# An attention kernel whose Gram rows are scaled by their diagonal, with the low parts of the diagonal blocks kept in one triangle

## What is computed

```python
q = heads(x @ W_q); k_t = heads(text_ehs @ W_k); v_t = heads(text_ehs @ W_v)
probs_t = softmax(einsum('bhsd,bhtd->bhst', q, k_t) * attn_scale)
text_out = einsum('bhst,bhtd->bhsd', probs_t, v_t)
qsem = l2norm(einsum('bhst,bte->bhse', probs_t, text_ehs))
sem = einsum('bhse,bne->bhsn', qsem, l2norm(ip_ehs))
probs_ip = softmax(q @ k_ip * attn_scale + 0.5 * sem) * spatial_mask
out = (text_out + probs_ip @ v_ip) @ W_out + b_out + x
```

## Time and profile before

| | us |
|---|---|
| median of 3 runs | 434.62 |
| lowest, highest | 431.41, 434.82 |
| the profiled execution | 431.83 |
| its span, first to last instruction | 430.0 |

### The profile page before, as it was taken

The page is one execution under the profiler, slowest core; times in us unless marked ns, Lnnn a source line. Parts: engine busy times, 40 slices in busy tenths (PEclk is TensorE's granted clock), DMA queues, the critical chain, the costliest instruction groups (busy, mean ns, idle before and its releaser), DMA issues.

```text
span 430.0 us, 9498 instructions
## 1 busy us (share of the span) xinstructions
PE 401.6 (93%) x3656; PEld 322.4 (75%) x3656; DVE 224.8 (52%) x482; ACT 204.3 (47%) x483; POOL 206.3 (48%) x218
## 2 busy tenths in 40 slices
PE   8999898899899999999999999999999899986786
PEld 5648678678788878887878788878888688864652
DVE  0893773656357635652666347544566366424232
ACT  1524125364555554656445645465553654473520
POOL 3020380354547543766268624963474328438351
PEclk9999999999999999999999999999999999999795
DMA  8499895066217320571147023712072100010000
GB/s 280 126 301 187 213 169 127 11 182 104 63 68 159 57 78 2 156 125 49 31 142 139 12 69 109 147 27 78 2 169 40 38 2 3 3 37 2 2 16 13
DMA packets 29455, 38.03 MB, mean 88 GB/s; under 512 B 14361, under 2 KB 26745, under 8 KB 28729
## 3 DMA queue, kind: packets, MB, share of 16 engines
q1 hardware_dynamic: 28514, 36.36, 35.7%
q10 hardware_dynamic: 896, 1.07, 0.8%
HBM read 28.50 MB, written 8.81 MB: 87 GB/s over the span
## 4 chain that ended last, share of the span: by engine, by line
PE 84%; ACT 4%; DVE 3%; DMA 3%; POOL 2%; issue 2%; SPq 1%; ACTq 0%; POOLq 0%; DVEq 0%
PE PR L883 41%; PE Y L883 26%; PE O L883 8%; PE P L883 8%; DMA et<-ctxT 2%; ACT big L666 1%; ACT er L670 1%; POOL pb L532 1%; DVE big L751 1%; POOL t L554 1%; ACT R L685 1%; PE PR L1042 1%; DVE mx L785 1%; DMA qst<-ma 0%; DVE el L725 0%
## 5 line engine op out<-in xcount | busy, mean ns | idle before, releaser
L532 POOL TENSOR_TENSOR pb<-pb 128x448 f32<-128x448 f32 x78 | 88.8, 1139 | 134.9 <-DVE pb L807 128.8
L785 DVE TENSOR_REDUCE mx<-PR 112x1 f32<-112x371 f32 x160 | 83.8, 539 | 85.1 <-PE PR L883 84.1
L883 PE MATMUL Y<-er,Gh 128*128 128x448 f32 x240 | 96.2, 401 | 5.6 <-ACT er L670 5.6
L807 DVE TENSOR_TENSOR pb<-big,Y 128x448 f32<-128x448 f32 x120 | 73.2, 621 | 38.9 <-PE Y L883 38.9
L883 PE MATMUL Y<-er,Gl 128*128 128x448 f32 x240 | 88.1, 367 | 0.0
L666 ACT ACTIVATE big<-P 128x448 f32<-128x448 f32 x120 | 65.0, 541 | 14.9 <-PE P L883 14.2
L670 ACT ACTIVATE er<-big 128x448 fp32r<-128x448 f32 x120 | 69.3, 578 | 3.8
L883 PEld LDWEIGHTS Y<-er,Gh 128*128 128x128 f32 x240 | 45.8, 191 | 20.4 <-DVE pb L807 11.1
L883 PE MATMUL PR<-kst,qst 96*112 96x371 bf16 x160 | 51.6, 331 | 3.0 <-DVE mx L785 2.0
L883 PE MATMUL P<-qst,kst 99*128 99x112 bf16 x480 | 41.7, 215 | 6.2 <-ACT big L666 5.9
L883 PEld LDWEIGHTS Y<-er,Gl 128*128 128x128 f32 x240 | 45.8, 191 | 2.1
(11 more groups left out here) (147 smaller groups left out, 660.3 us busy)
## 6 DMA issues: line engine op xcount, KB each, us to landing
et<-ctxT SPq DMA_DIRECT2D x8, 752.0 KB, 4.6
kst<-kd SPq DMA_DIRECT2D x7, 720.0 KB, 7.4
kd<-ks SPq DMA_DIRECT2D x16, 288.0 KB, 2.9
qst<-qd SPq DMA_DIRECT2D x48, 70.0 KB, 2.5
kst<-kd SPq DMA_DIRECT2D x7, 480.0 KB, 9.3
kst<-kd SPq DMA_DIRECT2D x9, 240.0 KB, 9.3
qd<-kst SPq DMA_DIRECT2D x4, 336.0 KB, 6.1
vx<-xr SPq DMA_DIRECT2D x8, 140.0 KB, 2.2
```

Of the source, the lines that this page charges most:

```text
L532: pool.tensor_tensor(total, total, (pz, pm)[j], ALU.add).then_inc(s_S, 1)
L785: dve.tensor_reduce(mx[b % 2][:, h:h + 1], bank[0:S, 0:T], AX.X, ALU.max).then_inc(s_free[seq[u] % NR], 1)
L807: dve.tensor_tensor((pz, pm, pa[g % 2])[j], eb[g % 3][:, 448 * j:448 * j + 448], Y[y % 2][:, 0:448], ALU.mult).then_inc(s_P, 1)
L883: return pe.matmul(o, st, mv, start=start, stop=stop, **kw)
```

## The change

The diagonal of each G block is taken first (c, at least 1e-30), row k of G is divided by c_k, and er becomes round(e * c). In a diagonal block the low parts of both triangles are gathered by symmetry into one triangle, rounded into Gh itself: so diagonal blocks need no Gl, and a gram has 5 + 3 + 1 = 9 matmuls. For this a G unit has two parts on DVE: a head (diagonal by a product with the identity and a sum, clamp, reciprocal) before ACT's rounding, and a part "Gl" behind it that also writes dj, the low parts above the diagonal; GpSimd halves the diagonal and clears one triangle of Gh ("U"), PE transposes dj into a further PR bank ("D", L1002 of the new file), and DVE adds the transposed block into Gh. ROUNDS moves one m and takes U0 to U2 and D0 to D2 in. usel's entry for the norm is 2.0 instead of 1.0. ident_d grows from 128x128 to 128x384 (identity and two triangle masks).

```diff
-          "S0 m g m K2 m S1 v m S2 G1 m",
-          "S0 m g T0 T1 m r0 G2 m S1 m pw v S2 m V0",
-          "Kr S0 r1 m g m V1 m S1 m m v r2 S2 mT z V2",
+          "S0 m g m U0 K2 m S1 v m D0 S2 G1 m",
+          "S0 m g T0 T1 m r0 U1 G2 m D1 S1 pw v S2 m m V0",
+          "Kr S0 r1 U2 m g m V1 m S1 m m v r2 D2 S2 mT z V2",
...
-    order += [("G", 0, i) for i in range(3)] + [("K", 1, c) for c in range(3)] + [("Kr", 1)]
+    order += [("G", 0, 0), ("G", 0, 1), ("U", 0, 0), ("D", 0, 0), ("G", 0, 2), ("U", 0, 1), ("D", 0, 1)]
+    order += [("K", 1, 0), ("U", 0, 2), ("D", 0, 2)] + [("K", 1, c) for c in (1, 2)] + [("Kr", 1)]
...
-    order += [("mT", 0)] + [("G", 1, i) for i in range(3)] + [("St", 0, c) for c in range(3)]
+    order += [("mT", 0)] + [("G", 1, 0), ("G", 1, 1), ("U", 1, 0), ("D", 1, 0), ("G", 1, 2), ("U", 1, 1), ("D", 1, 1)]
+    order += [("St", 0, c) for c in range(3)] + [("U", 1, 2), ("D", 1, 2)]
...
+                if u[0] == "U":
+                    b, i = u[1], u[2]
+                    w = ROWS[i]
+                    diag = Gh[b % 2][0:w, GOFF[i]:GOFF[i] + w]
+                    pool.wait_ge(s_ru, 3 * b + i + 1)
+                    pool.tensor_tensor(diag, diag.bitcast(f32), half_upper[0:w, 0:w], ALU.mult).then_inc(s_gu, 1)
...
-                    filled(act, u)
+                    act.wait_ge(s_gd, 3 * b + i + 1)
...
+                    w = T - 128 * i
+                    act.activation(Gh[b % 2][0:r, GOFF[i]:GOFF[i] + w], bank[0:r, 0:w], ACT.Copy, scale=grc[b % 2][0:r, i:i + 1])
...
-                    act.activation(er[g % 2][:, 448 * c:448 * c + 448], e, ACT.Copy).then_inc(s_er, 1)
+                    act.activation(er[g % 2][:, 448 * c:448 * c + 448], e, ACT.Copy,
+                                   scale=gc[g // NG % 2][:, c:c + 1]).then_inc(s_er, 1)
...
                     if b == 0:
                         dve.wait_ge(s_set, FILLS)
+                        dve.wait_ge(s_w, 16 * FIRST)
+                    if b >= 2:
+                        dve.wait_ge(s_gram, 3 * NG * (b - 1))
+                    filled(dve, u)
+                    c = gc[b % 2][0:r, i:i + 1]
+                    link(dve.scalar_tensor_tensor(dj[i][0:r, 0:r], bank[0:r, 0:r], 1.0, ident[0:r, 0:r], ALU.mult, ALU.mult,
+                                                  accum_out=c))
+                    link(dve.tensor_scalar(c, c, TINY, None, ALU.max))
+                    dve.reciprocal(grc[b % 2][0:r, i:i + 1], c).then_inc(s_gd, 1)
+                elif k == "Gl":
+                    b, i, r = u[1], u[2], ROWS[u[2]]
+                    bank = PR[seq[("G", b, i)] % NR]
                     dve.wait_ge(s_gh, 3 * b + i + 1)
...
+                    low.then_inc(s_free[seq[("G", b, i)] % NR], 1)
+                    freed(dve, seq[("G", b, i)])
+                    dve.scalar_tensor_tensor(dj[i][0:r, 0:r], dj[i][0:r, 0:r], c, upper[0:r, 0:r], ALU.mult,
+                                             ALU.mult).then_inc(s_ru, 1)
+                elif k == "D":
+                    b, i, r = u[1], u[2], ROWS[u[2]]
+                    filled(dve, u)
+                    dve.wait_ge(s_gu, 3 * b + i + 1)
+                    diag = Gh[b % 2][0:r, GOFF[i]:GOFF[i] + r]
+                    dve.scalar_tensor_tensor(diag, bank[0:r, 0:r], grc[b % 2][0:r, i:i + 1], diag.bitcast(f32), ALU.mult,
+                                             ALU.add).then_inc(s_free[seq[u] % NR], 1)
...
+                elif k == "D":
+                    b, i, r = u[1], u[2], ROWS[u[2]]
+                    pe.wait_ge(s_ru, 3 * b + i + 1)
+                    pe.transpose(bank[0:r, 0:r], dj[i][0:r, 0:r], ident[0:r, 0:r]).then_inc(s_ring, 1)
...
-                        mm(d, Gh[b % 2][:, o:o + 128], mv, i == 0, False)
-                        last = mm(d, Gl[b % 2][:, o:o + 128], mv, False, i == j)
+                        last = mm(d, Gh[b % 2][:, o:o + 128], mv, i == 0, i == j)
+                        if i < j:
+                            o = LOFF[i] + 128 * (j - i - 1)
+                            mm(d, Gl[b % 2][:, o:o + 128], mv, False, False)
```

More of the change, by code:

```diff
@@ L21 @@
 GOFF = (0, 384, 640)
+LOFF = (0, 256)
+TINY = 1e-30
 STACK = ((0, 3), (1, 2), (2, 1))
-FILLS = 17
+FILLS = 19
 FIRST, REST = 2, 6
@@ L95, in master_schedule @@
                 unit.update({"G0": ("G", n, 0), "G1": ("G", n, 1), "G2": ("G", n, 2)})
+                unit.update({"U0": ("U", n, 0), "U1": ("U", n, 1), "U2": ("U", n, 2)})
+                unit.update({"D0": ("D", n, 0), "D1": ("D", n, 1), "D2": ("D", n, 2)})
             if n + 1 < B:
@@ L124, in behind @@
     for u in order:
-        if u[0] in ("K", "G") and u[1] >= 2:
+        if u[0] == "G" and u[1] < 2:
+            out += [u, ("Gl",) + u[1:]]
+        elif u[0] == "G":
+            out, held = out + held + [u], [("Gl",) + u[1:]]
+        elif u[0] == "K" and u[1] >= 2:
             out, held = out + held, [u]
@@ L128, in behind @@
             out.append(u)
-            if u[0] in ("max", "gram", "mT", "o"):
-                out, held = out + held, []
+        if u[0] in ("max", "gram", "mT", "o"):
+            out, held = out + held, []
     return out + held
-RING = ("K", "G", "V", "T", "pT", "cT", "o", "max", "mT", "vW", "vWo")
+RING = ("K", "G", "D", "V", "T", "pT", "cT", "o", "max", "mT", "vW", "vWo")
 NR = 3
@@ L177, in build @@
         Gh = [sb(f"Gh{i}", [128, 768], f32r) for i in range(2)]
-        Gl = [sb(f"Gl{i}", [128, 768], f32r) for i in range(2)]
+        Gl = [sb(f"Gl{i}", [128, 384], f32r) for i in range(2)]
+        gc = [sb(f"gc{i}", [128, 3]) for i in range(2)]
+        grc = [sb(f"grc{i}", [128, 3]) for i in range(2)]
+        dj = [sb(f"dj{i}", [128, 128]) for i in range(3)]
         Vt = [sb(f"Vt{i}", [128, 3, H, MV]) for i in range(2)]
@@ L192, in build @@
         mask_s = sb("mask_s", [S, 1])
-        ident = sb("ident", [128, 128])
+        masks = sb("masks", [128, 3 * 128])
         ones = sb("ones", [128, S])
@@ L214, in build @@
         res = [sb(f"res{i}", [S, C]) for i in range(2)]
+        ident, half_upper, upper = [masks[:, 128 * i:128 * i + 128] for i in range(3)]
         vrT = et[:, 0, 0:H * NIP * 3].rearrange("p (c n) -> p c n", c=3)
@@ L276, in build @@
         s_pad = sem("s_pad")
+        s_gd = sem("s_gd")
         s_gh = sem("s_gh")
+        s_ru = sem("s_ru")
+        s_gu = sem("s_gu")
         s_ms = sem("s_ms")
@@ L375, in _ @@
                   (wvip_s, wvip.rearrange("(c p) n -> p c n", p=128))]
-            first = [(kst[0][96:99, :, :], krow.rearrange("r (h t) -> r h t", h=H)), (ident[:, :], ident_d)]
+            first = [(kst[0][96:99, :, :], krow.rearrange("r (h t) -> r h t", h=H)), (masks[:, :], ident_d)]
             rest = [(hv[:, :], hm_v), (mask_s[:, :], mask), (bias[:, :], bout.partition_broadcast(S))]
@@ L490, in _ @@
             fill(usel[:, :], 0.0)
-            fill(usel[:, 21:22], 1.0)
+            fill(usel[:, 21:22], 2.0)
+            for i in range(2):
+                fill(gc[i][:, :], 1.0)
             fill(half[:, :], 0.5)
@@ L781, in _ @@
-                    low.then_inc(s_free[seq[u] % NR], 1)
+                        dve.wait_ge(s_w, 16 * FIRST)
[6 more added lines that the diff above has]
+                    link(dve.tensor_scalar(c, c, TINY, None, ALU.max))
@@ L1001, in _ @@
                     if j == 2 and r == 0:
-                        freed(pe, seq[("G", b, 2)])
+                        for i in range(3):
+                            freed(pe, seq[("D", b, i)])
                     if j == 2:
```

22 lines of the change are left out of this document (8 added, 14 removed).

## The result

The changed kernel takes 462.82 us (median of 4 runs, 458.06 to 465.84), the kernel before 434.72 beside it: ratio 1.062, interval 1.051 to 1.073. Forecast were 453 us, in a range of 436 to 467. The profiled execution took 458.06 us, the lowest of the four, its span 456.3 against 430.0.

The account below looks back on a forecast made before the run. PE was taken to bound the kernel, busy 93% of the span. +14.6 + 3.1 + 7.0 - 2.0 - 2.2 = +20.5 us on the profiled 431.83 gave 452.3, stated as 453 for the median, range 436 to 467.

Parts of the forecast that it names:

- first term: First maximum in batch 0's prologue, delayed by the wait for masks, the G units' chain and half clock: +14.6 us.
- third: Six batches with G units in their rounds, +1.17 us each: +7.0 us, bounds -10 to +13.
- The gram: One matmul less per j saves 0.40 us a gram, not 0.60, since j = 0 waits for DVE's product.
- Prologue, batch 0: DVE's head waits for masks landing about 46.5 us, PE's clock drops: first maximum +14.6 us, bounds 12 and 18.
- Prologue, batch 1: ACT has G2's rounding ahead of its first exponential, which starts 3.1 us later; bounds 2 and 5.
- Batches 1 to 6: Waits behind G0, G1 and G2 outweigh shorter grams: +1.17 us a batch, +7.0 us in all.
- Batch 0: No G units in its rounds, so five grams each save 0.40 us: -2.0 us.
- Batch 7 and tail: Four grams on the chain, one at half clock: 3 x -0.4 and -1.0, -2.2 us.
- (a): Rival: DVE's and ACT's new work hides wholly, prologue too, only PE counts: 13.1 us saved, 418.7 us; chance 6%.
- (b): Rival: prologue costs as forecast, but the rounds gain all of the saving: 436.4 us; chance 13%.
- (c): Rival: masks land as DVE reaches them, so the prologue costs the chain alone, some 4 us: 442 us; chance 10%.
- (d): Rival: same mechanism, heavier: head at 1.05, clock low for longer, er on ACT's chain: 464 us; chance 10%.

Follow-up runs that it names:

- Nine alone: The kernel before with the three Gl matmuls on the diagonal blocks left out of every gram, nothing else changed: 420.48 us against 433.83, ratio 0.968.
- second prologue: Changed kernel with masks early, batch 0's U right behind its G units, two scores ahead of batch 1's G2, rounds as in the changed kernel: 451.05 us.
- last version: Changed kernel with masks early, Gl of G0 and G1 behind the first product, D1 behind V0, prologue ordered again: 438.72 us, ratio 1.0097.

## Why the prediction was right

The sign, the mechanism and the two places held; the sum was 5.7 us too small (20.5 forecast, 26.2 in the span). Against the median of all runs, 462.8, the forecast of 453 was 9.8 too low. 4 us of that come from the step between the two: the profiled execution of the changed kernel lay about 1% under the median, and the forecast's own 0.6% on 452.3 would have given 455, not 453. That the sum came so near has some luck in it, since the first term was too large while the third was too small. By its steps:

- **The gram**: worth 0.40 with DVE in time. Nine alone gave 0.35 on average, because DVE's queue ahead of the product holds back r0 (K) and r1 (G0's Gl part and a maximum). In r0 of the changed kernel it is 0.21. The row from which 0.40 was read is such an r0: K's rest on DVE ends 0.21 ahead of the product there, and the step left it out.
- **Prologue, batch 0**: +14.6 forecast, +12.3 measured. The masks landed at 44.0, not 46.5, and the clock was back at 51.6, not 54. 1.6 us of the 12.3 lie ahead of the first G unit (it began at 34.97 instead of 33.4, with the clock low from 31.1 to 34.6 in that execution) and belong to no step.
- **Prologue, batch 1**: +3.1 forecast, +4.3 measured up to the first gram. The step itself was right: from the transpose of the maxima to the first exponential it is 8.43 us (75.92 to 84.35) instead of 5.54, +2.9. The other 1.5 lie between this exponential and the gram, where the clock is at 0.50 from 82.3 to 89.2; the forecast had no low clock there.
- **Batches 1 to 6**: +7.0 forecast, +13.1 measured, 0.1 over the upper bound of +13. This is the mis-sized term: 2.2 us a batch instead of 1.17. By rounds of batch 3: r0 -0.21 instead of -0.40; r1 +1.18 instead of +0.90, of which the gram behind G0 is +1.06 (0.78 forecast); r2 +1.76 instead of +1.35, the gram behind G1 +0.83 (0.57) and what follows it +0.93 (0.78); r3 -0.18 instead of -0.28; r4 -0.40, as forecast. The head was right (0.71 for 0.75). Short were the operations with a column as scalar (0.05 to 0.07 each, three behind each G unit), some 0.2 of the 0.28 missing behind G0; the rest is not resolved further. That DVE's queue ahead of the product is the cause is shown by the run with Gl behind it, and that D1's bank is 0.62 of r2 by the run with D1 later.
- **Batch 0** -2.0 forecast, -0.6 measured. K on DVE takes 0.2, as in nine alone (-1.8), and er's longer copy 0.4, by the run without scale. The largest part is in its last round, where PE waits 0.72 us for the DMA of batch 1's maxima. The kernel before and nine alone have no such wait, and the versions of the change have it with 0.72 to 0.90; why the maxima come later was not tried:

```profile
123.44 0.55 PE L926 MATMUL P<-qst,kst 99*128 99x112 bf16 x8 [0.72 <-DMA qst<-ma]
```

- **Batch 7 and tail** -2.2 forecast, -2.9 measured, most of it not from shorter grams: the kernel before ran its last units at half clock from 421 us on, the changed kernel did not until its last 2 us. So the agreement is luck.
- **The signs named beforehand**: PE idle from 38.7 to 46.7 (37 to 49 forecast), L799 at 44.0 (46 to 47), clock at 0.50 from 41.4 to 51.6 (42 to 54), first maximum at 56.2 (57 to 59), first exponential 2.9 later (3), waits for L850 of 1.57 and 1.34 (1.0 to 1.2), the other grams 2.2 to 2.5 to the next unit (2.2).
- **The pages.** The pointer's price of the Trainium skill (ScalarE: Activation LUTs, "What ACT_TABLE_LOAD costs"), 93 ns, agrees with 0.669 against 0.577 us; of the estimated 2.2 us for the whole the traces show 1.2, where the sum had taken 0. That a sum counts as a second instruction, as the Trainium skill has it (VectorE: DVE Perf Modes, "Two Vector instructions with no wait between them") agrees too: it has a row, of 0.08 us, and puts 0.12 on the head instead of 0.2.
- **The rivals.** (a) falls: DVE's free time was not where it was needed. (b) falls by the table of rounds. (c) falls: the load landed 6 us after DVE was ready. (d), with 464, was nearer to the 462.8 of the median than the forecast was, and its weights were partly right: low clock in more places and heavier DVE operations, but not the head of 1.05; er's copy was half of the 2.4 it gave.

## What to carry to other kernels

Before taking work from the busiest engine, write down what it waits for at the very place, and what stands ahead of that on the other engine: here a third of the saving went into a wait at once, and new DVE work ahead of one product cost more than the matmuls saved. Of a new wait on a load, look up when the load lands, not when it is first needed: a constant that had almost 20 us to spare (it lands at 44 to 45 us, and its first use was at 63.7) became a 6 us stop of DVE, and more through the ring of banks and then the clock. Waits in a row hide one another, so removing one shows the next; try them together before judging any.

## What was not expected of the hardware

- Low clock follows a short wait in one execution and not in another. The kernel before and nine alone have the same prologue, and in both PE waits 1.8 us for a maximum (50.39 and 50.26). In the first the clock stays full behind it, in the second it is at half from 50.8 to 54.2 us. PE in both, and the stretch behind (columns as in rows 10), the kernel before first:

```profile
50.39 0.81 PE L883 MATMUL PR<-kst,qst 96*112 96x371 bf16 x2 [1.83 <-DVE mx L785]
50.80:54.20 3.40, 3.36 (x26) 3.27 (x26) 1.72 (x4) 0.44 (x1) 0.06 (x1) 1.00 0.61 155
...
50.26 0.94 PE L883 MATMUL PR<-kst,qst 96*112 96x371 bf16 x2 [1.84 <-DVE mx L785]
50.80:54.20 3.40, 3.40 (x14) 3.35 (x15) 0.96 (x2) 0.00 (x0) 0.00 (x0) 0.51 0.53 133
```

And in the run with early masks the clock stayed at 0.50 to 48.1 us, though PE was busy for all 6.00 us from 42 on. Executions of the changed kernel spread over 7.8 us (458.06 to 465.84), those of the kernel before beside them over 4.5. That the phases with low clock make this spread was not tested.
- One profiled execution, that of the changed kernel with the second prologue, took 715.9 us where the kernel's other three took 448 to 455. Its granted clock reads 1.00 throughout (columns as in rows 10):

```profile
400.00:500.00 100.00, 99.81 (x555) 72.11 (x554) 33.26 (x86) 34.70 (x73) 34.37 (x36) 1.00 0.17 40
```

PE was busy all the time, its matmuls of 448 columns started 0.41 us apart instead of 0.20, its grams took 3.2 to 3.6 us instead of 1.9 to 3.5, a round of batch 3 14 to 18 us. What slowed it the page does not show, and it stays open; it was seen once.
- Partly open is what keeps the first gram of the last version 8.2 us behind the kernel before. 2.3 of it lie ahead of the first G unit (35.72 for 33.41, clock low from 31.4 to 34.9), 2.1 from there to the first maximum, and 3.8 behind it, where PE waits 2.06 us for the low parts of G2 of batch 1 and the clock is at 0.50 from 75.8 to 82.7:

```profile
76.80 0.51 PE L1005 MATMUL PR<-masks,dj 115*115 115x115 f32 x1 [2.06 <-DVE dj L819]
```

How much of this is the chain through DVE, ACT and DVE and how much the clock was not tried.
